# A normalization step of the next sample, moved by half a slot on VectorE

## What is computed

```python
x = x + attn(layernorm(x), ...)     # 4 layers, below
x = x + ffn(layernorm(x), ...)      # 16 experts, top 4, and a shared one

h = layernorm(x)
for l in range(4):
    xn = ln(h, ln1_w[l], ln1_b[l])
    a = attention(xn, Wq[l], Wk[l], Wv[l], Wo[l], u_bias[l])
    h = h + a
    fn = ln(h, ln2_w[l], ln2_b[l])
    h = h + gelu(fn @ W1[l].T + b1[l]) @ W2[l].T + b2[l]
```

## Time and profile before

| | |
|---|---|
| median of 3 runs | 2553.26 us (2552.2 to 2553.8) |
| the profiled execution, its own time | 2553.8 us |
| its span in the profile | 2551.8 us |
| granted TensorE clock, mean | 0.994 |
| PE busy | 2417.8 us, 95% |
| DVE busy | 2075.5 us, 81% |
| ACT busy | 1854.8 us, 73% |
| POOL busy | 1172.9 us, 46% |

### The profile page before, as it was taken

How to read it: one execution, slowest core, us unless ns; L and a number is a source line. 1 busy time by engine, 2 the same in 40 slices (tenths; PEclk the granted TensorE clock), 3 DMA queues, 4 the chain that set the end, 5 groups by cost and what they waited for, 6 DMA issues and landing times. The chain is left out here.

```text
span 2551.8 us, 80664 instructions
## 1 busy us (share of the span) xinstructions
PE 2417.8 (95%) x31360; PEld 1980.5 (78%) x31360; DVE 2075.5 (81%) x5069; ACT 1854.8 (73%) x2837; POOL 1172.9 (46%) x2091
## 2 busy tenths in 40 slices
PE   3899999999999999999999999999999999599998
PEld 2678787888888888888888888888888887477776
DVE  5898889888888888888888888888888885477775
ACT  2577777778777777878787777877787777455554
POOL 5445554545444444445444454454444442233332
PEclk9999999999999999999999999999999999799999
DMA  6222323223332333222333333222332231100000
GB/s 190 81 84 77 89 80 86 82 79 86 85 86 81 89 87 85 82 83 84 85 87 86 85 86 86 83 81 83 85 86 82 84 86 31 41 26 26 26 22 17
DMA packets 221129, 195.88 MB, mean 77 GB/s; under 512 B 28880, under 2 KB 217424, under 8 KB 220752
## 3 DMA queue, kind: packets, MB, share of 16 engines
q1 hardware_dynamic: 220752, 190.73, 26.6%
HBM read 14.46 MB, written 4.19 MB: 7 GB/s over the span
## 5 line engine op out<-in xcount | busy, mean ns | idle before, releaser
L818 DVE TENSOR_REDUCE rowmax<-bank 128x4 f32<-128x1024 f32 (+1 forms) x768 | 937.1, 1220 | 253.5 <-PE bank L466 253.5
L639 ACT ACTIVATE probs<-bank 128x1024 f32<-128x1024 f32 x768 | 786.6, 1024 | 394.3 <-PE bank L509 388.5
L466 PE MATMUL bank<-kstack,qstack 62*128 62x128 f32 (+1 forms) x4096 | 435.0, 305 | 0.0
L509 PE MATMUL bank<-qstack,kstack 64*128 64x256 f32 (+1 forms) x4096 | 432.5, 304 | 0.0
L678 ACT ACT_TABLE_LOAD x256 | 328.4, 1283 | 4.5
L466 PEld LDWEIGHTS bank<-kstack,qstack 62*128 62x128 f32 x4096 | 314.6, 193 | 0.0
L509 PEld LDWEIGHTS bank<-qstack,kstack 64*128 64x128 f32 x4096 | 312.6, 191 | 0.0
L455 PE MATMUL bank<-mask_half,pick_half 64*128 64x128 bf16 (+1 forms) x3072 | 268.8, 243 | 33.4 <-DVE rowmax L818 21.8
L528 PE MATMUL bank<-probs,v_pad 128*32 128x256 f32 x4096 | 275.0, 386 | 1.5 <-ACT probs L639 1.5
L588 PE MATMUL bank<-w,hidden 128*128 128x128 f32 x2048 | 271.1, 276 | 0.9 <-ACT hidden L687 0.9
L498 PE MATMUL bank<-maskT_half,pick_half 64*128 64x128 bf16 (+1 forms) x3072 | 268.7, 243 | 1.9 <-ACT probs L639 1.9
(11 more groups left out here) (144 smaller groups left out, 5306.5 us busy)
## 6 DMA issues: line engine op xcount, KB each, us to landing
qstack<-base SPq DMA_DIRECT2D x768, 128.0 KB, 2.4
kstack<-base SPq DMA_DIRECT2D x384, 128.0 KB, 2.4
turn_x<-turn_c SPq DMA_DIRECT2D x512, 32.0 KB, 1.9
qstack<-maxrows SPq DMA_DIRECT2D x256, 16.0 KB
xin<-in_x SPq DMA_DIRECT2D x16, 256.0 KB, 3.0
out<-ot SPq DMA_DIRECT2D x16, 256.0 KB, 2.4
h_all<-in_x SPq DMA_DIRECT2D x2, 512.0 KB, 5.4
w<-in_w SPq DMA_DIRECT2D x4, 256.0 KB, 3.8
```

The lines of the kernel that those rows point to most:

```text
L466: last = pe.matmul(bank[:, b, i * wide:(i + 1) * wide], qstack[rows, r, p0 + i, t * 128:(t + 1) * 128], kstack[rows, r, p0 + i, 0:wide], s ...
L509: last = pe.matmul(bank[:, 2 + b, i * wide:(i + 1) * wide], kstack[rows, r, p0 + i, kt * 128:(kt + 1) * 128], qstack[rows, r, p0 + i, q0:S ...
L639: act.activation(probs[:, (ROUNDS * n + k) % PR], bank[:, 2:4, :], ACT.Exp, scale=SCALE).then_inc(exp_done, 1)
L818: dve.tensor_reduce(rowmax[:, t, :, p0:p0 + heads], bank[:, 0:2, :].rearrange("p b (h c) -> p b h c", h=heads), AX_X, ALU.max).then_inc(ma ...
```

## The change

`apply_1` is called in round 2 of the slot, for unit s+1, and no longer in round 5 for unit s+2. For a unit n this is the move from round 5 of slot n-2 to round 2 of slot n-1, half a slot later. On DVE it now stands behind `max_round` 2 and ahead of `apply_0` and `max_round` 3. No instruction is added or removed.

```diff
                         split_rest(s)
+                    if k == 2 and live(s + 1):
+                        apply_1(s + 1)
                     if k == 3 and live(s - 4):
                         divide(s - 4)
                     if k == 2 and s % PER == 0 and LN0_FIRST <= s // PER + 2 < B // PER:
                         apply_0(s // PER + 2)
...
                     if k == 5 and live(s - 6):
                         resid_2(s - 6)
-                    if k == 5 and live(s + 2):
-                        apply_1(s + 2)
                     if k == 5 and live(s - 2):
                         maxrows_out(s - 2)
```

## The result

The changed kernel takes 2571.89 us (median of 4 runs, 2570.55 to 2574.56) against 2553.53 us for the kernel before, measured beside it: a ratio of 1.007, 95% interval 1.0058 to 1.0083. That is 18.4 us slower. The forecast was 11.7 us slower, with a range up to 2569 us; the direction is right and the size is not.

A forecast was written before the change was run, and what follows sets the result against it. A ring of DVE and PE bounds rounds 2 and 3, PE alone round 5. Slots with `apply_0` 10.3 + 0.5, first slots 0.85, ordinary slots 0: 11.7 us slower, 2565.0 us, range 2559 to 2569.

The forecast's parts named there:

- Round 5, worth nothing: DVE in round 5: removing `apply_1` takes away 0.92 us but gains nothing, as the `maxrows` copy waits for PE's `m1`.
- The ordinary slot, hidden: Round 2 without `apply_0`: the moved pair fits DVE's idle time before maximum 3, 0.25 us to spare, cost 0.
- Rival C: Ordinary slots lose their cover too: 0.14 us in 113 slots on top of the main forecast, 2581 us; chance 0.07.
- Slots with `apply_0`, 0.94 us each from POOL's hold: Round 2, slots 6 to 26: POOL instructions hold DVE's six, maximum 3 comes 0.94 us later; 11 slots, 10.3 us.
- Rival B: POOL doesn't hold the moved instructions as replayed: 12 x 0.51 + 0.85 = 7.0 us, 2560.3 us; chance 0.14.
- Slot 4: Slot with `apply_0` where no POOL instruction stretches L743: the moved pair costs only 0.51 us.
- PE is waiting in that time, so all of it stays: Slots with `apply_0`: `f1` is done while maximum 3 is late, so the whole 0.94 us delay lengthens the slot.
- The first slots, 0.85 us: Slots 0 to 2: `f1(2)` 0.5 us later, slot 2's `apply_0` another 0.51, less about 0.16; together 0.85 us slower.

The follow-up runs named there:

- the seventh experiment: Against the kernel before, `apply_1` still in round 5: `apply_0` moved from round 2 to round 5, behind `apply_1`; 2545.78 us, ratio 0.9968.
- the second: Against the changed kernel: `apply_1` back in round 5 of the slot before, only for slots that have `apply_0`; 2553.73 us, ratio 0.9998.
- the fifth experiment: Against the changed kernel with `apply_0` moved to round 5 (2544.86 us): one unused `tensor_scalar` added behind `apply_1` in slots 28 to 127; 2555.86 us.
- the third experiment: Against the changed kernel: POOL's add of row b_o (L975) moved from round 3 to the end of round 4 in slots with `apply_0`; 2561.80 us.
- fourth: Against the changed kernel: 12 unneeded PE transposes behind `f1` in the 11 slots 6 to 26 with `apply_0`; 2564.68 us, ratio 1.0047.
- sixth: Against the changed kernel: two more unused `tensor_scalar` instructions on DVE ahead of `apply_0` in the 11 slots 6 to 26; 2583.08 us, ratio 1.0118.

## Why the prediction was wrong

**Round 5, worth nothing: right.** The idle time ahead of the copy grew to 1.02 us (1.1 forecast), and the slot's time didn't change.

**The ordinary slot, hidden: right.** The second instruction of the pair got through ahead of POOL's L943, as in slot 10 of before. The 0.9 us over 99 slots are within what the profiles differ by: the same slots take 16.401 us in the kernel before, 16.410 in the changed kernel, 16.418 in the seventh experiment, which doesn't have the change, and 16.434 in the second, which has it in all of them and yet takes as long as the kernel before. Rival C (0.14 us in each) did not come, and the fifth experiment shows that it was one instruction away.

**Slots with `apply_0`, 0.94 us each from POOL's hold: right.** Measured 0.94 in seven of the 11, with maximum 3 at 3.78 or 3.79 us in all of them; and where POOL's L975 is taken away, 3.36 against 3.35. Rival B (0.51 us each) falls with the third L743 of slot 10, held across the seam until L975 is done, and with the third experiment. Slot 4 cost 0.51 us, as forecast. The Trainium skill (page "SBUF — State Buffer", section "Who interferes with whom") has the rule that fits, `tensor_scalar` blocked while GpSimd holds the shared port pair, and the stretched L743 and L884 agree. Its other half, that a VectorE instruction issued first holds GpSimd, doesn't show: in slot 10 of the changed kernel L767 runs until 190.29, L943 starts at 190.20, 1.63 us behind maximum 2, and takes 0.40 us; in the ordinary slot before, with no such instruction ahead of it, it also starts 1015.12 - 1013.49 = 1.63 us behind maximum 2 and takes 0.40.

**"PE is waiting in that time, so all of it stays": the step that failed.** It counted PE's wait as lost time alone, and took PE's work behind the wait at its full speed. The trace before shows no low clock in a slot of this stage, where PE's longest wait was 0.87 us in slots 6 to 26 and 1.24 us in slot 4, and the forecast had no term for it. The wait of 1.79 us brought it in four of 11 slots, 5.9 us together, which is most of the 6.7 us by which the measured time lies above the forecast. Experiments 3, 4 and 6 change PE's idle time in three ways (shorter by POOL's order, filled by PE, longer by DVE) and the low clock goes, goes and spreads. The Trainium skill's page "TensorE: Matmul & The Clock Gate" (section "Part 1: The HAM clock gate") says that activity is what keeps TensorE at 2.4 GHz, with 1.2 GHz as the default. The trace agrees, with 0.51 granted behind the wait and 1.00 around it; read as a rule that speaks against this change, it would have called for a rival of its own.

**The first slots, 0.85 us: mis-sized by about a microsecond, with the other sign.** The first maximum was 0.6 us late (44.83 us, 0.5 forecast), but PE's first score matmuls of slot 2 ran fast in the changed kernel. First the kernel before, then the changed one:

```profile
45.51 0.40 PE L455 MATMUL bank<-mask_half,pick_half 64*128 64x256 bf16 x2 [0.17 <-DVE rowmax L818]
...
46.11 0.28 PE L455 MATMUL bank<-mask_half,pick_half 64*128 64x256 bf16 x2 [0.21 <-DVE rowmax L818]
```

The changed kernel's record has the clock at 1.00 from 45.7 to 49.1 us and at 0.50 until 79.9; that of the kernel before begins only at 80.6 us. Why the matmuls ran fast in one profile and slow in the other wasn't tried, so the -0.3 us is no more than what came out of two profiles. The third, fourth and sixth experiments, which have the changed kernel's code up to slot 3, reach slot 4 at 81.47, 81.48 and 80.21 us, against 80.55 in the changed kernel and 80.86 before: a term of 0.85 us is smaller than this scatter. The forecast also left out the `apply_0` of slot 0 in its count.

**The sum.** 11.7 us forecast; 1.15 less for the first slots (-0.3 and not 0.85), 5.9 more for the clock and 0.9 for the ordinary slots make 17.35. Measured is 17.8 on the profiled spans, with the 0.5 us named above left over, and 18.4 on the medians. The medians less the 5.9 us for the clock give 12.5 us, near the 11.7 forecast, in part since the first slots erred one way and the ordinary slots and the rest the other.

What stays open is which of the 11 slots get the low clock. They do the same work with the same wait to 0.02 us (1.79 to 1.81), and nothing in their rows tells slot 6 from slot 10. So the number of slots hit, four or seven, is measured and not derived.

## What to carry to other kernels

When a moved instruction lands in a slot that is already late on that engine and that the next engine waits for, the whole of it is paid, and instructions behind it can move into the reach of a neighbour that holds them: replay the slot instruction by instruction, against the other engine's rows. Then add a second term for what the wait does to TensorE's speed, not only for how long it lasts; here a wait that grew from 0.9 to 1.8 us brought the low clock to slots that had none. And look at the rare slots first: 12 of 128 held nearly the whole effect of this change, and moving their extra work to where the engine idles gained 9.0 us with the change and 7.6 us without it.

## What was not expected of the hardware

Twelve transposes that nobody reads, put into PE's wait in 11 slots, made the changed kernel faster, from 2571.9 to 2564.7 us, since with 0.50 us of idle time in place of 1.79 the granted clock stayed at 1.00. And `bn_stats` beside a running GpSimd instruction keeps its 0.29 us, where a `tensor_scalar` of the same input at the same place goes from 0.34 to 0.47 us.
